# One core, a message-passing layer: two more tiles are gathered row by row, by ScalarE's queue, and two fewer by GpSimd

## What is computed

```python
h = jnp.maximum(_layernorm(x, axis=-1), 0.0)
# per edge, from edge_attr_8: a small MLP gives 256 weights
w = silu(silu(edge_attr_8 @ W1 + b1) @ W2 + b2) @ W3 + b3
# per edge: products of h[src] (8 scalars, 8 vectors), edge_attr_4 and w
m0 = ALPHA * (einsum('eu,euw->ew', hs_e * sh0, W00) + INV_SQRT3 * einsum('eui,ei,euw->ew', hv_e, sh1, W110))
m1 = ALPHA * (einsum('eu,ei,euw->ewi', hs_e, sh1, W01) + einsum('eui,euw->ewi', hv_e * sh0, W10))
agg = segment_sum(concatenate([m0, m1]), dst, num_segments=100000) / sqrt(16)
x = x + h_self(h, Ws, Wv) + agg          # h_self: 8x8 maps of scalars and vectors of every node
```

## Time and profile before

| | |
|---|---|
| median of 3 runs | 610.87 us (608.48 to 611.92) |
| the profiled execution | 610.19 us, of which the span of the trace is 608.4 |
| granted PE clock, mean | 0.817 |
| busy | PE 86%, POOL 80%, DVE 68%, ACT 67% |
| POOL's operations | 186 gathers, 196 scatters |
| rows gathered by SP | 1192 |
| end of the node part | 180 us |

### The profile page before, as it was taken

One profiled execution on the slowest core, in us unless ns is written; L12 is line 12 of the kernel. 1 busy time (PEld: TensorE's weight loads), 2 busy tenths in 40 slices (PEclk: granted clock), 3 DMA queues, 4 the chain that ended last, 5 costly groups with the idle time before them and its releaser, 6 DMA issues.

```text
span 608.4 us, 13260 instructions
## 1 busy us (share of the span) xinstructions
PE 522.6 (86%) x3255; PEld 414.2 (68%) x3255; DVE 412.1 (68%) x1142; ACT 405.7 (67%) x1215; POOL 486.0 (80%) x391
## 2 busy tenths in 40 slices
PE   5877988888978797599999899999899999959790
PEld 4776777776865674577777677776676777736590
DVE  5686777777785775477787767777777587643820
ACT  3433555454556785589998888988888698847430
POOL 6777777777777777888888888888888888888777
PEclk9968999998988787587888788889886778866555
DMA  4654765655641111222222222222222222222222
GB/s 129 190 157 123 196 171 173 182 169 153 193 122 15 14 15 14 10 10 11 11 10 10 12 11 9 12 10 11 12 9 11 10 12 10 11 10 10 8 10 9
DMA packets 54262, 34.40 MB, mean 57 GB/s; under 512 B 37830, under 2 KB 41656, under 8 KB 54200
## 3 DMA queue, kind: packets, MB, share of 16 engines
q0 software_dynamic: 34176, 6.28, 20.2%
q1 hardware_dynamic: 12854, 14.63, 8.3%
q10 hardware_dynamic: 7170, 12.81, 5.7%
HBM read 17.59 MB, written 16.08 MB: 55 GB/s over the span
## 4 chain that ended last, share of the span: by engine, by line
SPq 62%; issue 16%; PE 8%; DVE 5%; DMA 4%; POOL 3%; ACT 1%; ACTq 0%; DVEq 0%
SPq L292 44%; SPq L288 12%; DMA xin<-in_x_dram 4%; POOL out_dram L332 3%; PE ps L713 2%; SPq L225 1%; SPq L275 1%; PE ps L616 1%; DVE oc L856 1%; DVE ps L848 1%; PE ps L586 1%; PE ps L610 1%; DVE ps L821 1%; PE ps L601 1%; PE ps L716 1%
## 5 line engine op out<-in xcount | busy, mean ns | idle before, releaser
L332 POOL DMA_INDIRECT out_dram<-sums,idx_i x196 | 306.3, 1563 | 62.0 <-issue 57.1
L319 POOL DMA_INDIRECT xg<-in_x_dram,src_all x186 | 178.8, 961 | 57.7 <-issue 56.4
L713 PE MATMUL ps<-msg,eq 128*128 128x32 f32 (+1 forms) x980 | 140.1, 295 | 13.1 <-DVE carry L993 11.2
L713 PEld LDWEIGHTS ps<-msg,eq 128*128 128x128 f32 x980 | 136.1, 217 | 14.0 <-DVE carry L993 11.6
L1017 DVE TENSOR_TENSOR prod<-ps,coef 128x256 f32<-128x256 f32 (+1 forms) x245 | 98.7, 470 | 16.6 <-PE ps L662 14.3
L486 ACT ACTIVATE dsq<-ps,dcol 128x512 f32<-128x512 f32 x196 | 87.7, 546 | 0.2 <-PE ps L675 0.2
L662 PE MATMUL ps<-w3blk,x 64*128 64x256 f32 x392 | 73.9, 509 | 0.0
L509 ACT ACTIVATE eq<-dsq,onecol 128x384 f32<-128x384 f32 x147 | 73.8, 528 | 0.0
L472 ACT ACTIVATE sums<-ps 128x132 f32<-128x132 f32 x49 | 13.7, 280 | 87.4 <-PE ps L716 64.5
L384 ACT ACTIVATE sqT<-ps 128x512 f32<-128x512 f32 (+2 forms) x50 | 29.3, 585 | 63.7 <-PE ps L601 63.4
L662 PEld LDWEIGHTS ps<-w3blk,x 64*128 64x128 f32 x392 | 44.6, 248 | 36.8 <-issue 31.8
(11 more groups left out here) (106 smaller groups left out, 832.6 us busy)
## 6 DMA issues: line engine op xcount, KB each, us to landing
xg<-in_x_dram SPq DMA_DIRECT2D x1192, 0.1 KB
xin<-in_x_dram SPq DMA_DIRECT2D x48, 256.0 KB, 2.8
out_dram<-oc ACTq DMA_DIRECT2D x48, 256.0 KB, 2.5
out_dram<-sums,idx_i POOLq DMA_INDIRECT x196, 3.1
xg<-in_x_dram,src_all POOLq DMA_INDIRECT x186, 2.5
er_all<-in_edge_attr_dram SPq DMA_DIRECT2D x1, 780.0 KB
sh_all<-in_edge_attr_dram SPq DMA_DIRECT2D x1, 390.0 KB
xin<-in_x_dram SPq DMA_DIRECT2D x1, 192.0 KB
```

The lines of the kernel that those rows point to most:

```text
L319: pool.indirect_dma_start(xg[:, t * D:(t + 1) * D], None, x, bass.IndirectOffsetOnAxis(ap=src_all[:, t:t + 1], axis=0)).then_inc(signal, 16)
L332: pool.indirect_dma_start(out, bass.IndirectOffsetOnAxis(ap=idx_i[:, k % NS, a:a + 1], axis=0), sums[:, k % NS, a * DR:a * DR + D], None, ...
L713: m = pe.matmul(psSUM[:, a * DR:a * DR + n], eq[:, k % 2, o:o + P], msg[:, k % 2, b, 0:n], start=(b == a), stop=(not carried and (b == a - ...
```

## The change

The constant `RT` goes from 10 to 12, so the tiles gathered by rows begin at `G1` = 184. POOL's loop runs to `G1`, so it gathers 184 tiles. A new bound, `G2` = `G1` + 2 = 186, divides the tiles that are gathered by rows: SP takes 186 to 195, as before, and ACT takes 184 and 185, 256 rows, through a `gather_rows` of its own. It is called at four places of each half pass with three rows each (in the first half, at three places). 256 rows are used up in the 22nd of 24 halves. All twelve tiles belong to the last late unit, and the unit before it, of 36 tiles, becomes one of 34. ACT's hardware loop over passes 3 to 10 becomes Python's, so that each place has rows of its own.

```diff
--- before.py
+++ after.py
@@ -63,8 +63,10 @@
 
 
 
-    GT, RT = 10, 10
+
+    GT, RT, RA = 10, 12, 2
     G1 = T + 1 - RT
+    G2 = G1 + RA
     EW = UT * NB
     GF = EARLY * GT
     PASSES = NU // 2
@@ -212,6 +214,8 @@
 
 
 
+        x_bytes = x.bitcast(u8).rearrange("n d -> (n d)").rearrange("(a n) -> a n", a=1)
+
         block = ctx.enter_context(nc.Block(no_gpsimd_drain=True))
 
 
@@ -275,8 +279,7 @@
                     sp.dma_start(row_i[:, (t - G1) * P:(t - G1) * P + n], rows_of).then_inc(row_loaded, 16)
             sp.dma_start(out[N:N + BT * P, :].rearrange("(p r) d -> p (r d)", p=P), spare0[:, :]).then_inc(s["spare_stored"], 16)
 
-            x_bytes = x.bitcast(u8).rearrange("n d -> (n d)").rearrange("(a n) -> a n", a=1)
-            late_rows = iter([(t, p) for t in range(G1, T + 1) for p in range(P if t < T else TAIL)])
+            late_rows = iter([(t, p) for t in range(G2, T + 1) for p in range(P if t < T else TAIL)])
             nodes = []
 
             def gather_rows(count):
@@ -428,6 +431,20 @@
                 if k >= NS:
                     act.wait_ge(s["sq_done"], q - NS + 2)
                 act.activation(dcol[:, k % NS, :], dst_f[:, ds(q * BT, BT)], ACT.Copy).then_inc(s["dcol_done"], 1)
+
+            rows_of_tiles = iter([(t, p) for t in range(G1, G2) for p in range(P)])
+            offsets = []
+
+            def gather_rows(count):
+
+                for t, p in itertools.islice(rows_of_tiles, count):
+                    if p % 32 == 0:
+                        o = (t - G1) * P + p
+                        _, offsets[:] = nc.values_load_multi_w_load_instructions(
+                            row_at[0:1, o:o + 32], engines=[mybir.EngineType.Activation], min_val=0, max_val=(N - 1) * D * 4,
+                            skip_runtime_bounds_check_because="src holds rows of x")
+                    act.dma_start(xg[p:p + 1, t * D:(t + 1) * D].bitcast(u8), x_bytes[:, ds(offsets[p % 32], D * 4)])\
+                       .then_inc(gathered_row[t - G1], 16)
 
             def store(c, base):
                 act.wait_ge(s["o_done"], c + 1)
@@ -511,6 +528,7 @@
                 m.then_inc(s["eq_done"], 1)
 
             act.wait_ge(s["w_loaded"], 16 * (2 + 8 + UT))
+            act.wait_ge(s["rows_at"], 2)
             for c in range(NCH - 2, NCH):
                 store(c, c)
             mlp_in(0, 0)
@@ -531,10 +549,12 @@
                     if not end:
                         mlp_in(u + 2, k + 2)
                     if not (first and h == 0):
+                        gather_rows(3)
                         copy_sums(q - 1, kq - 1)
                     if h == 0 and last:
                         feat_square(squares, width(squares))
                     dst_square(q + 1, kq + 1)
+                    gather_rows(3)
                     if h == 0 and not last and roots is not None:
                         feat_std(roots, width(roots))
                     if not end:
@@ -558,7 +580,7 @@
             edge_pass(0, True, False, EARLY - 1, EARLY)
             edge_pass(1, False, False, EARLY, EARLY + 1)
             edge_pass(2, False, False, EARLY + 1)
-            with act.Fori(3, PASSES - 1) as v:
+            for v in range(3, PASSES - 1):
                 edge_pass(v, False, False)
             edge_pass(PASSES - 1, False, True, EARLY + 2, EARLY + 2)
             copy_sums(NQ - 2, NQ - 2)
```

## The result

The changed kernel took 615.5 us, the median of 8 runs (612.91 to 617.86), against 610.21 for 8 runs of the kernel before (608.48 to 611.92): a ratio of 1.0067, with a 95% interval of 1.004 to 1.0094. The number lies in the range on record (605.5 to 619), 3.1 us above the forecast of 612.4 and 1.5 us above the forecast's own range (609 to 614). The ratio of a run, as it is on record, need not equal the quotient of its two medians.

What follows compares the result with a forecast made beforehand. The prediction took SP's last row, then the slow last pass, then POOL's three batches as the bound. 610.19 - 0 + 1.56 + 0.4 + 0 = 612.15, or 612.8 against the median, gave 612.4, range 605.5 to 619.

Steps and rivals of the forecast that it cites:

- ACT exposed: Rival in the edge passes: ACT does not hide its rows, 2.35 us per batch exposed, 646, middle case 620; chance 0.17.
- long register loads: Rival on ACT: register loads take three times SP's, 6.4 us each, adding 3.0 us at the end, 614.8; chance 0.06.
- within 0.5%: Outcome for the whole kernel: time between 607.8 and 613.9, no telling from no change; chance 0.60.
- The bound: End of the kernel: SP's rows landed, then 44 us of a slow last pass, then three batches of POOL.
- Which pause of POOL hangs on it: POOL's late scatters: the 1.22 us before batch 46 waits for DVE's indices; POOL alone would be 0.92 us earlier.
- POOL, 2.53 us off its queue: POOL's gathers: two fewer save 2.53 us, which turns into a longer wait before batch 46, counted as 0.
- SP, +1.56 us: SP's start: two more loads of row numbers cost 1.4 us, the longer conversion 0.16, delaying SP's last row.
- A wider last unit, +0.4: DVE and ACT in the last pass: 12 tiles instead of 10 lengthen five steps behind the landing, 0.4 us.
- ACT's rows at nothing: ACT in the edge passes: 256 rows and eight loads add about 19 us, hidden by waits, so costed at nothing.
- the cover: ACT's 42.5 us of waits for PE and POOL plus 10.7 us at DVE's row wait, 53 us to absorb ACT's work.
- The sum: Whole kernel: 610.19 - 0 + 1.56 + 0.4 + 0 = 612.15, or 612.8 against the median; 612.4 predicted.
- POOL alone as the bound: Rival at the end: last pass 5.4 us quicker, POOL alone sets the end, 606.7 or 605.5; chance 0.17.

Runs made afterwards that it cites:

- e4: The change with SP's tiles by rows cut to 8, POOL gathering 186 and ACT 2: 608.1 us against 610.68 for the kernel before, ratio 0.994.
- e12: The change with 9 tiles on SP, 3 on ACT and ACT's square root earlier in the last pass: 604.67 us against 610.78 for the kernel before.
- e6: The change with ACT's square root for the last unit one step earlier in the last pass, on a held-up chip: 839.97 us, ratio 0.9938.
- e10: The change with ACT's square root one step earlier in the last pass, repeated on another held-up chip: 839.97 us, ratio 0.9941.
- e1: The kernel before with row numbers of two more tiles loaded and converted on SP's side, never used: 612.16 us against 610.68, ratio 1.0024.
- e2: The kernel before with only ACT's loop over passes 3 to 10 unrolled: 611.84 us, ratio 1.0002.
- e3: The change with row numbers of ACT's two tiles loaded by ACT's queue instead of SP's: 612.98 us, ratio 1.0026 to the kernel before.
- e8: The change with 8 tiles on SP, 4 on ACT, whose queue loads its row numbers, on a held-up chip: 844.42 us, ratio 0.9976.

## Why the prediction was right, and where it was not

The number was in range, but by luck in part: it lies above the forecast's own 609 to 614, in the part of the range that was put there for ACT exposed (620) and for long register loads (614.8), and neither came about. The most likely case, "within 0.5%", is missed by the middle of the ratio.

**The bound.** SP's last row, then the last pass, then POOL: right. The chain, the wait of 17.88 us behind a row DMA, e4 (SP relieved, ACT and its rows kept, 2.6 us faster than before) and e12 show it from both sides, and e6 and e10 show that the last pass passes a delay on.

**Which pause of POOL hangs on it.** Wrong. I took the 1.57 us before batch 44 for a pause of POOL's own, since the profile names a DMA as its releaser, and only the 1.22 us before batch 46 for a wait for DVE. The timeline of before, 560 to 600, has DVE's indices of batch 44 here:

```profile
568.10 0.15 DVE L1007 TENSOR_TENSOR idx_i<-idx_f,trash 128x4 int32<-128x4 f32 x1
```

They are done at 568.25, and POOL goes on at 568.53, 0.28 us later, the same 0.28 as behind the indices of batch 46 (584.11 and 584.39). So POOL was 2.2 us ahead, not 0.92, the extra wait appeared before batch 44 (8.31 us) and not before batch 46 (1.22 in both), and POOL alone would have been 608.0; e4 measured 608.1. (A batch of four scatters comes to 7.47 us by the prediction's own rows, 4 x (1.563 + 0.305), not 7.43; nothing in its sum hangs on that.)

**POOL, 2.53 us off its queue.** Right that it turns into waiting. On the queue it was 1.23 us in this profile.

**SP, +1.56 us.** Right in kind, and e1 gives 1.5 us by the ratio; but the profile of the change shows 4.9 us at the last row. This is the mis-sized term. In that profile the part that the prediction costed is 1.46 us (x taken up 1.32 later, the conversion 0.14 longer). The rest had been put at nothing: 1.43 with PE's lower clock in the node steps ahead of the conversion, 0.38 in SP's register load behind it, and 1.6 between the first row and the last. None of these is shown to be a cost of the change: e2, with SP's program as it was, has a stretch of 1.6 us more ahead of the conversion, a register load of 2.46 us, and 2.2 us more between first and last row.

**A wider last unit, +0.4.** Right: 0.52.

**ACT's rows at nothing.** Right. Bare rows cost no idle at either kind of place. The loads were costed at 2.1 us behind squares and 1.1 ahead of a copy, 14.8 in all; they left six holes of 1.1 to 1.2 us behind squares and none ahead of a copy, 7.1 in all. I expected ACT's slack to fall from 42.5 to some 25 us, and DVE's wait for the rows to fall to 3 to 8 us. Instead PE's part of ACT's waits grew from 30.2 to 34.5 us, and DVE was ready 3.6 us sooner. So the cover was not used up by the rows as I had it, and a wait for PE is not slack that simply adds up. That DVE was sooner isn't a gain of the change either: in e4, with the same rows on ACT, it came to its last unit at 533.34, 2.1 us later than before.

**The sum.** 1.56 + 0.4 = 1.96 us was forecast for the profiled execution, 5.65 measured, and the difference lies in the 5.10 us up to DVE's resuming. The comparison of medians says 5.3, the ratio 4.1, and e1 and e3 together 3.1, with 1.9 and 1.7 us either way. That SP's start costs more than 2 us on average is therefore not shown; that the change costs 0.4% or more is shown on the one chip of the first comparison. On the two chips with the hold-up it was 1.000 and 1.0015.

**Rivals.** POOL alone as the bound: it is what e4 and e12 reach, but only with fewer rows on SP. ACT exposed: not with 256 rows, nor with 384; with 512 the time is 22.3 us longer than with 384, and e8's trace leaves open whether ACT or PE's lower clock is behind it. Loads three times as long on ACT: they took 2.13 to 2.31 us there, as on SP. (The rival's 614.8 leaves out the 0.4 of the wider unit; with it, it is 615.2.) The page "Runtime: NRT & Kernel Launch" of the Trainium skill gives some 200 ns per register (section "Instruction fetch mechanics"), and the page's loads are from HBM; the loads of this kernel read SBUF, and 32 registers in 2.2 us are 69 ns each, on both engines.

## What to carry to other kernels

When two chains end within some two microseconds of each other, work has to be taken off both. This change took two tiles off POOL and gave SP, the later of the two, a little more; taking two tiles off SP instead (e4), or one off SP besides POOL's two (e12, with the early root), is what made the kernel faster. Rows issued by a busy engine's sequencer cost nothing here as long as they fitted into the lead of the sequencer over its engine, which can be read from the times of its register instructions; a register load behind the squares left 1.1 to 1.2 us of idle each time. Where a short wait has a DMA as its releaser, look at what else the waiting instruction needs before calling it the engine's own. And a microsecond or two between two profiles is not yet a cost of the change: lay the same chain out for several traces first.

## What was unexpected of the hardware

The same program of SP began its rows anywhere between 48.4 and 50.8 us (before, e2, e3), with the granted clock of PE in 42 to 48 at 1.00, 0.65 and 0.57. Two of the four chips of the experiments held every kernel up in the node part until POOL's gathers were over, some 230 us, while POOL gathered at its usual 0.96 us; its cause is open. A row DMA took 0.23 us to issue on ACT as on SP, and SP's 373.5 to 374.8 us for its rows behind the last x load don't tell the kernels with rows on ACT's queue from those without.
